# Turning the first tiles one by one behind nine matrix products of zeros, and a norm moved behind the last silu and product of a shared stage

## The reference

```python
x = L0_attn_hidden_states                      # (2, 512, 256)
x = x + _L0_attn_ref(_layernorm(x), ...)       # q, k, v = silu(conv4(h @ W)); l2norm; delta rule; rmsnorm; gate; Wo
x = x + _L0_ffn_ref(_layernorm(x), ...)        # top 2 of 8 experts, and a shared expert of width 704
x = x + _L1_attn_ref(_layernorm(x), ...)       # rotary, softcap 30 by tanh, causal softmax, Wo
x = x + _L1_ffn_ref(_layernorm(x), ...)        # top 6 of 16 experts

def _layernorm(x, axis=-1, eps=1e-05):
    m = jnp.mean(x, axis=axis, keepdims=True)
    v = jnp.var(x, axis=axis, keepdims=True)
    return (x - m) / jnp.sqrt(v + eps)
```

## Time and profile before

| what | value |
|---|---|
| median of 3 runs | 845.69 us (845.59 to 847.47) |
| the profiled execution | 841.79 us, its span 840.0 us |
| PE busy | 786.3 us (94%), 4825 instructions |
| DVE busy | 482.3 us (57%), 1166 instructions |
| ACT busy | 361.3 us (43%), 756 instructions |
| POOL busy | 218.0 us (26%), 318 instructions |
| granted PE clock, mean | 0.994 |

### The profile page before, as it was taken

How to read it: one execution, slowest core, us unless ns; L and a number is a source line. 1 busy time by engine, 2 the same in 40 slices (tenths; PEclk the granted TensorE clock), 3 DMA queues, 4 the chain that set the end, 5 groups by cost and what they waited for, 6 DMA issues and landing times.

```text
span 840.0 us, 14393 instructions
## 1 busy us (share of the span) xinstructions
PE 786.3 (94%) x4825; PEld 544.4 (65%) x4825; DVE 482.3 (57%) x1166; ACT 361.3 (43%) x756; POOL 218.0 (26%) x318
## 2 busy tenths in 40 slices
PE   5988799879989998899999999989999999999998
PEld 3576566666657785677777767766764545455557
DVE  5999866766522225866565565767755463324443
ACT  3988767646123333352332342323246676211111
POOL 3644654111610034111111111116712233200000
PEclk9998999999999999999999999999999999999999
DMA  4001780092343322034442322212333433294431
GB/s 144 2 1 31 231 292 2 2 229 79 107 144 102 101 69 68 21 104 121 144 131 68 101 68 68 76 39 92 113 82 114 134 95 116 73 289 127 126 126 50
DMA packets 95807, 85.72 MB, mean 102 GB/s; under 512 B 34792, under 2 KB 84456, under 8 KB 95736
## 3 DMA queue, kind: packets, MB, share of 16 engines
q1 hardware_dynamic: 88200, 70.05, 28.7%
q0 software_dynamic: 4224, 11.74, 4.1%
q10 hardware_dynamic: 3312, 3.02, 1.1%
HBM read 57.02 MB, written 26.71 MB: 100 GB/s over the span
## 4 chain that ended last, share of the span: by engine, by line
PE 75%; DVE 10%; ACT 7%; issue 4%; DMA 1%; POOL 1%; SPq 0%; ACTq 0%; another core or an unknown queue 0%; DVEq 0%; POOLq 0%
PE bank L1488 9%; PE bank L1451 7%; PE bank L1306 6%; PE bank L1345 6%; PE bank L1267 6%; PE bank L1283 6%; PE bank L1331 5%; PE bank L730 4%; PE bank L756 3%; PE bank L953 3%; PE bank L2309 3%; PE bank L975 2%; ACT arena L2366 2%; PE bank L2266 2%; PE bank L2293 2%
## 5 line engine op out<-in xcount | busy, mean ns | idle before, releaser
L1607 ACT ACTIVATE arena<-bank 128x512 f32<-128x512 f32 (+1 forms) x96 | 46.9, 525 | 147.4 <-PE bank L1451 135.2
L1229 POOL TENSOR_TENSOR arena<-arena,causal_t 128x256 f32<-128x256 f32 x64 | 45.2, 726 | 215.9 <-ACT arena L1612 215.9
L1488 PEld LDWEIGHTS bank<-arena 128*128 128x128 f32 x640 | 76.1, 191 | 4.8 <-POOL arena L1229 3.5
L1488 PE MATMUL bank<-arena 128*128 128x129 f32 x640 | 77.2, 275 | 1.9 <-POOL arena L1229 1.9
L1451 PE MATMUL bank<-arena 128*128 128x512 f32 (+3 forms) x256 | 74.6, 434 | 1.4 <-DVE arena L1685 1.4
L1540 ACT ACTIVATE arena<-bank 128x512 f32<-128x512 f32 (+1 forms) x39 | 20.2, 520 | 123.3 <-PE bank L1267 106.9
L1306 PE MATMUL bank<-arena 128*128 128x256 f32 (+1 forms) x272 | 66.2, 382 | 4.4 <-DVE arena L1665 2.7
L1267 PE MATMUL bank<-xnT,arena 128*128 128x512 f32 (+1 forms) x168 | 65.9, 514 | 0.0
L1306 PEld LDWEIGHTS bank<-arena 128*128 128x128 f32 (+1 forms) x272 | 50.9, 190 | 22.6 <-issue 13.2
L1345 PE MATMUL bank<-arena 128*128 128x256 f32 x256 | 61.0, 381 | 2.5 <-DVE arena L1692 2.0
L1345 PEld LDWEIGHTS bank<-arena 128*128 128x128 f32 x256 | 48.1, 190 | 23.3 <-issue 12.0
(11 more groups left out here) (296 smaller groups left out, 1486.7 us busy)
## 6 DMA issues: line engine op xcount, KB each, us to landing
arena<-in_w_gu SPq DMA_DIRECT2D x44, 256.0 KB, 3.3
rows_in<-place SPq DMA_DIRECT2D x5, 1664.0 KB, 14.4
arena<-in_w_dn SPq DMA_DIRECT2D x34, 128.0 KB, 3.5
rows<-arena SPq DMA_DIRECT2D x8, 544.0 KB, 4.3
arena<-in_w_dn SPq DMA_DIRECT2D x24, 176.0 KB
arena<-in_wq SPq DMA_DIRECT2D x32, 128.0 KB
arena<-in_wo SPq DMA_DIRECT2D x32, 128.0 KB
arena<-rows SPq DMA_DIRECT2D x32, 128.0 KB, 2.1
```

The lines of the kernel that those rows point to most:

```text
L1229: nc.gpsimd.tensor_tensor(blocks, blocks, causal_t[:].unsqueeze(1).to_broadcast([P, 2, P]), ALU.mult).then_inc(s_p, 1)
L1488: mm = nc.tensor.matmul(b_o[pair][:, t * (DH + 1):(t + 1) * (DH + 1)], pr[:, o:o + P], v[:, grp, kt, :], start=(kt == 0), stop=(kt == qb))
L1607: nc.scalar.activation(th[:, sbank * 512:sbank * 512 + w], b_s[sbank][:, 0:w], ACT.Tanh, scale=SCALE / SOFTCAP).then_inc(s_th, 1)
```

## The change

Four edits. First, `pe_turn` waits for one tile at a time and turns its two blocks, one into each of the two banks; both banks are complete only with the fourth tile. Second, POOL sets 384 columns of the arena (`still`) to zero, and PE begins with nine products of them, 128 x 256 outputs, into bank 7, before it looks for the identity or a tile. Third, on ACT `ready(Sqrt)` and std 5 move from behind silu 14 to behind silu 16; the rest keeps its order. Fourth, on DVE `ln_norm(5)` moves from behind the product of step 15 to behind that of step 16.

```diff
             def pe_turn(self, pe, half):
-                pe.wait_ge(ln_xn, 4 * (half + 1))
-                for k in range(KD):
-                    q = half * KD + k
-                    for j in range(4):
-                        mm = nc.tensor.transpose(bank[q][:, j * P:(j + 1) * P],
+                for j in range(4):
+                    pe.wait_ge(ln_xn, 4 * half + j + 1)
+                    for k in range(KD):
+                        mm = nc.tensor.transpose(bank[half * KD + k][:, j * P:(j + 1) * P],
                                                  xn[:, half * 4 + j, k * P:(k + 1) * P], ident[:])
-                    mm.then_inc(ln_tp, 1)
-
+                        if j == 3:
+                            mm.then_inc(ln_tp, 1)
+
+        still = arena[:, ARENA - 3 * P:]
...
             pool.memset(warm[:, 0:2], 0.0).then_inc(s_eps, 1)
+            pool.memset(still, 0.0).then_inc(s_eps, 1)
             attn0.pool(pool)
...
         def _(pe):
+            pe.wait_ge(s_eps, 3)
+            for _ in range(9):
+                nc.tensor.matmul(bank[7][:, 0:256], still[:, 0:P], still[:, P:3 * P], start=True, stop=True)
             pe.wait_ge(s_id.sem, 16)
...
                 if M == F0END - 4:
                     self.ready(ACT.Sqrt)
                     self.ln_std(act, 4)
-                if M == F0END - 3:
+                if M == F0END - 2:
+                    self.ln_evac(act, 4)
+                if M == F0END - 1:
                     self.ready(ACT.Sqrt)
                     self.ln_std(act, 5)
-                if M == F0END - 2:
-                    self.ln_evac(act, 4)
             self.ln_evac(act, 5)
             self.ready(ACT.Tanh)
...
-                if M == F0END - 2:
+                if M == F0END - 1:
                     self.ln_norm(dve, 5)
```

## The result

| | change | before, same session | ratio (95%) |
|---|---|---|---|
| runs of the case | 839.21 us (837.31 to 840.47, 4 runs) | 845.98 us (845.59 to 847.47, 4 runs) | 0.9916 (0.9896 to 0.9937) |
| the change once more | 837.80 us (836.53 to 843.60, 12 runs) | 845.24 us (840.79 to 850.04, 18 runs) | 0.9930 (0.9906 to 0.9954) |
| the profiled execution | 837.31 us, span 835.5, mean clock 0.994 | 841.79 us, span 840.0, mean clock 0.994 | |

Faster by 6.8 us (5.3 to 8.8), where 5.3 were forecast. The two profiled executions are only 4.5 apart, and these 4.5 can be followed on the chain. They are read first.

What follows compares the result with a forecast made beforehand. PE, busy for 94% of the span, was taken to bound the kernel. Gains of 0.8 + 1.75 + 1.7 + 1.1 = 5.35, taken as 5.3, gave 845.7 - 5.3 = 840.4 us (range 839.3 to 841.6; 80%: 836.8 to 843.8).

Steps and rivals of the forecast that it cites:

- Zeros, turns and copies: Kernel start: first projection begins at 9.9 instead of 10.75, 0.8 us gained (bounds 0.5 and 1.1).
- the two ends that were worked out: Kernel start: products of zeros end at 6.8 or 8.1, by how soon the clock rises.
- The clock: First projection: eight passes at the high clock take 3.5 us instead of 5.26, 1.75 us gained.
- its example of up to 14: Skill page cited for the start: low-clock products vary from run to run of one kernel, 6 to 14.
- The clock falling again: Rival, 13%: clock drops between zeros and projection; four passes run low, 1.75 is gone, total 842.1 us.
- Slower: Rival, 3%: at the start, products of zeros don't raise the clock; 1.1 us slower, 846.8 us.
- The norm behind the silu: End of shared stage: silu 15 no longer waits behind std 5; keys start 1.7 us earlier (bounds 1.2 and 2.0).
- The table load: First attention head: Exp's table load moves ahead, off the chain; 1.1 us gained (bounds 0.9 and 1.28).
- no transfer is waited for there: Work after the start: follows PE without waiting for transfers, so the start's 2.55 us gain holds.
- the forecast's own signs of being wrong: Passes 0.85 apart in the first projections, keys less than 3 us earlier, or total falling by less than 3.
- 80% range: Whole kernel: 836.8 to 843.8 us, covering rivals in part and a microsecond of scatter between medians.
- More than that: Rival, 9%: the earlier chain misses the low clock from 51.5 to 54.5, 1.7 us more gain, 838.7 us.

Runs made afterwards that it cites:

- zeros-only kernel: Against before: only the nine products of zeros added, turns by halves and end of the shared stage as before; 842.26 us, ratio 0.9975.
- turns-only trace: Against before: only the turns made tile by tile, no products of zeros, end of the shared stage as before; 844.12 us, ratio 0.9992.
- the halves: Against before: the two edits at the start alone, 841.96 us (0.9988), and the two at the end of the shared stage alone, 841.12 us (0.9963).

## Why the prediction was right, point by point

**Zeros, turns and copies: 0.8 forecast, 1.0 measured.** The projection starts at 9.71, forecast 9.9. The products of zeros end at 7.79, between the two ends that were worked out (6.8 and 8.1). The weights' landing was said to be next in line, with 0.7 of cover: the projection started 0.04 behind the copies in six of the seven chains with nine products. In the change repeated, the earliest, it was 0.11, and the weights had landed at 9.3 for a projection at 9.43, so there the cover was used up. What the step had wrong is its reason: turning tile by tile was priced as part of it, and the zeros-only kernel starts its projection at 9.81 all the same. The gain is turns at the high clock. The turns didn't come in pairs behind each tile either.

**The clock: 1.75 forecast, 1.56 measured between the two profiles.** Passes 0.43 apart from the first, in all seven profiles with nine products. Eight at the high clock take 3.70 and not the 3.5 of the sum. Against other kernels that start as before it is more, since before's own profile is a mild case. The eight passes took 5.26, 5.45, 5.86, 5.92, 6.38 and 6.59 in the six without nine products. At 0.43 above 3.70 for each low one that is 4 to 7 low passes. The forecast's sentence on Part 1 of "TensorE: Matmul & The Clock Gate" in the Trainium skill, that the number of low products varies from run to run, is borne out by these six, four of which (5.26, 5.45, 5.86, 6.59) have the same start; its example of up to 14 wasn't met, and eight low ones, which would have made this term 3.5, neither. This is the likeliest reason why the start is worth more than 2.55 in the traces: the delta rule's first turns, at 55.1 us in before's profile, start at 52.0 to 52.8 with nine products of zeros and at 55.1 to 56.4 with none.

**The clock falling again: didn't happen.** The rival of 13% had PE with little but eight turns between the zeros and 9.9. The clock stayed up in all seven. Part 4 of that page of the Trainium skill, by which turns don't count as products do, would have made this rival the likely one, and these rows speak against it as far as this gap goes. It is a weak test: from the zeros to the projection it is 1.9 us, with eight turns in it, and even 2.5 us of idling at head 24 brought no low stretch in five of twelve. But neither did eight turns alone raise it: in the turns-only trace they run from 7.17 and the records begin at 15.5. *Slower* needed that zeros don't raise the clock; they do, by 4.5 to 6.5 us.

**The norm behind the silu: 1.7 forecast, 1.8 between the two profiles, 1.05 between the others.** The order of events was as worked out: silu 15 first, DVE's statistics next, gaps of 0.16 and 0.33 where 0.3 was forecast. The root ended at 322.08, before DVE was free for it at 322.28. What was over-sized is the starting point. The 2.34 us of idling that the sum took away is a property of that one execution; in four other kernels with the old order it is 1.6. The term came out at 1.05, under its bounds of 1.2 and 2.0: the order of events was right and the size wrong.

**The table load: 1.1 forecast, 1.7 between the two profiles, 1.2 to 1.3 between the others.** The 1.7 is 16.8 - 15.1, and the 16.8 is before's own, where other kernels have 16.4. In before's profile DVE's first rotation of the keys starts 2.5 us behind the first product of the keys, and 2.1 behind it in the twelve others; no row says why. The lower value is the one to trust. The forecast took PE's gap of 1.10 as the bound; the measured value is nearer to the load's 1.28, still inside its bounds.

**What was left out: "no transfer is waited for there".** It was said of the start, and nothing later was priced at all. Between the two ends the path has a wait for a transfer, present before the change as well, and mostly with a low stretch, which this execution of before happened not to have. Between the two profiles it took 2.5 of the 3.5 gained by then (1.0 left at 308 us): 0.8 in the wait, and in two groups of slow products alone (1.81 - 1.38) + (1.92 - 1.03) = 1.3. With 2.6 + 1.8 + 1.7 = 6.1 gained at the two ends and 4.5 left at the end of the span, 1.6 was lost in between. That is a loss against an execution of before that had luck there, and not one that the change makes. It is also why one of the forecast's own signs of being wrong was met, by a tenth: the keys were to start at 323.6 and at least 3 us earlier, and started at 324.96, 2.9 earlier.

**The sum.** 5.3 forecast. 4.5 between the profiles; 6.8 between the medians, 7.4 when repeated; 5.1 at equal clock (843.6 - 838.5), and 5.0 as the sum of the halves. So the forecast's mechanism gives its number once the clock is held equal, and in part by luck: the norm was over-sized by 0.65, and the start (2.6 to 3.2 in the traces, where it ends) and the load were under-sized by up to about as much. The stated range, 839.3 to 841.6, is a little wider than its bounds give (6.1 and 4.35 of gain, 839.6 and 841.35), and the first median lies 0.1 below its lower end, inside the 80% range. The further 1.7 to 2.3 of the medians goes with fewer or shorter low stretches in the change's runs (mean clock 0.9892 against 0.9878). Whether the edits cause that or the runs happened so stays open. *More than that*, the low stretch of 51.5 us missed by an earlier chain, didn't come: the profile after has one at 40.2 and another at 74.3, before at 51.5 and 75.4, with 10.2 us of low clock in all in each.

## What to carry to other kernels

An engine that would wait for its first data can be made to run products of nothing, if there are enough of them that its clock is up before the real work starts: nine moved the first projection's passes to 0.43 us, four left them at 0.85. When two profiles are to be compared, look up first whether low-clock stretches stand in one and not in the other, and price a wait by several executions and not by one. And look for short waits behind long lists of issues: here four pairs of transfers ahead of an urgent one cost 3 to 4 us, about half of what the change brought.

## What the runs showed of the hardware

- A wait of PE at the fourth routed block was followed by 3.4 or 6.8 us at half clock in all nine profiles in which it lasted 3.0 to 3.5 us, and not in the one with 2.5 (before's); with 0.6 us or less it didn't happen in three of three. The wait of 2.5 us at head 24 was followed by it in seven of twelve.
- Other low stretches, beginning at 40 to 52 and at 73 to 78 us, stood in all thirteen profiles whatever the edit; further ones, beginning at 88 to 105 or at 184, in six.
- While the clock's records haven't begun, the windows show 1.00, though passes are 0.85 apart. The spacing of the weight loads has to be read instead.
- A load of activation tables takes 1.28 us, and the activation behind it starts 0.02 later. On the chain it cost 1.2 to 1.3.
